# Moving the edge arrays' loads and packing ahead in the prologue of a four-layer graph network, and storing the packed edge table from the ScalarE queue

## The reference

```python
# layer 0: messages, mean over incoming edges, update
msgs = maximum(concat([h[src], h[dst], edge_attr]) @ mW1 + mb1, 0) @ mW2 + mb2
agg  = segment_sum(msgs, dst) / clip(count(dst), 1)
upd  = maximum(concat([h, agg]) @ uW1 + ub1, 0) @ uW2 + ub2 + h
x    = x + layernorm(upd) * gamma + beta
# layer 1: sum over neighbours;  layer 2: weighted GCN;  layer 3: APPNP step
x = x + h @ W1 + b1 + segment_sum(h[src], dst) @ W2 + b2
x = x + segment_sum(norm * (h @ W)[src], dst) + bias
x = x + h + relu(0.9 * segment_sum(norm1 * h[src], dst) + 0.1 * h)
```

## Time and profile before

| | |
|---|---|
| median of 3 runs | 1050.0 us (1049.88 to 1053.69) |
| the profiled execution | 1055.58 us, of which the span of the trace is 1053.7 us |
| PE busy | 877.1 us (83% of the span) |
| DVE busy | 645.6 us (61%) |
| ACT busy | 503.3 us (48%) |
| POOL busy | 495.6 us (47%) |
| DMA, mean over the span | 160 GB/s, 169.02 MB |

### The profile page before, as it was taken

One profiled execution on the slowest core, in us unless ns is written; L12 is line 12 of the kernel. 1 busy time (PEld: TensorE's weight loads), 2 busy tenths in 40 slices (PEclk: granted clock), 3 DMA queues, 4 the chain that ended last, 5 costly groups with the idle time before them and its releaser, 6 DMA issues.

```text
span 1053.7 us, 21016 instructions
## 1 busy us (share of the span) xinstructions
PE 877.1 (83%) x7797; PEld 792.2 (75%) x7797; DVE 645.6 (61%) x1759; ACT 503.3 (48%) x1012; POOL 495.6 (47%) x496
## 2 busy tenths in 40 slices
PE   4422887888778787888898888899899999999997
PEld 3422777777777776777887888788788988889786
DVE  5524676867776677667777777787775231213664
ACT  3211455655555555565666666676334300111874
POOL 6457665666666677566666666533411000003111
PEclk9566899999999999999999999999999999999999
DMA  5641355555655558555555555545623787786410
GB/s 145 193 135 45 96 147 147 151 151 149 202 160 147 147 139 138 160 152 157 153 152 148 155 159 153 143 144 169 187 62 141 283 306 285 292 304 206 136 54 23
DMA packets 118795, 169.02 MB, mean 160 GB/s; under 512 B 17248, under 2 KB 85382, under 8 KB 118691
## 3 DMA queue, kind: packets, MB, share of 16 engines
q1 hardware_dynamic: 104405, 138.82, 42.7%
q0 software_dynamic: 13648, 28.21, 10.9%
q10 hardware_dynamic: 638, 0.61, 0.3%
HBM read 109.15 MB, written 58.44 MB: 159 GB/s over the span
## 4 chain that ended last, share of the span: by engine, by line
PE 76%; issue 10%; DMA 4%; DVE 3%; another core or an unknown queue 2%; POOL 2%; ACT 2%; SPq 0%; ACTq 0%; DVEq 0%
PE ps L1883 13%; PE ps L1868 12%; PE ps L1740 12%; PE ps L1706 9%; PE ps L1720 9%; PE ps L1707 8%; PE ps L1738 4%; DMA edge_windows<-room 2%; PE ps L1693 2%; PE ps L1852 2%; POOL h L763 1%; PE ps L1755 1%; DMA x<-in_x 1%; DMA room<-dst_row 1%
## 5 line engine op out<-in xcount | busy, mean ns | idle before, releaser
L784 POOL DMA_INDIRECT room<-p_rows,idx x416 | 413.1, 993 | 235.2 <-issue 99.5
L1740 PE MATMUL ps<-room 128*128 128x100 bf16 x2400 | 193.8, 208 | 59.0 <-issue 57.5
L1740 PEld LDWEIGHTS ps<-room 128*128 128x128 bf16 x2400 | 152.0, 98 | 83.4 <-issue 79.2
L947 ACT ACTIVATE room<-ps 128x400 uint8<-128x400 f32 x200 | 101.1, 506 | 219.1 <-remote 209.6
L1706 PE MATMUL ps<-room,ident 128*128 128x128 f32 x832 | 172.0, 289 | 32.4 <-ACT g L922 15.4
L1738 PE MATMUL ps<-room 128*128 128x100 bf16 x800 | 155.6, 209 | 31.8 <-issue 29.2
L1707 PE MATMUL ps<-room 128*128 128x128 f32 x832 | 164.6, 280 | 0.4 <-issue 0.2
L1286 DVE TENSOR_TENSOR room<-room,Wp 128x800 bf16<-128x800 bf16 x300 | 156.4, 575 | 0.0
L1706 PEld LDWEIGHTS ps<-room,ident 128*128 128x128 f32 x832 | 129.8, 197 | 35.1 <-issue 31.3
L1279 DVE TENSOR_TENSOR room<-iota_k,Kt 128x800 bf16<-128x800 bf16 x100 | 57.4, 574 | 134.6 <-remote 134.4
L1883 PE MATMUL ps<-room,h 128*128 128x256 f32 (+1 forms) x650 | 136.2, 371 | 0.0
(11 more groups left out here) (195 smaller groups left out, 1096.9 us busy)
## 6 DMA issues: line engine op xcount, KB each, us to landing
weight_blocks<-room SPq DMA_DIRECT2D x100, 400.0 KB
room<-weight_blocks SPq DMA_DIRECT2D x12, 3200.0 KB
room<-dst_row SPq DMA_DIRECT2D x104, 128.0 KB
room<-count_blocks SPq DMA_DIRECT2D x8, 1600.0 KB
count_blocks<-room SPq DMA_DIRECT2D x100, 100.0 KB
room<-p_rows,idx POOLq DMA_INDIRECT x416
first_c<-count_blocks SPq DMA_DIRECT2D x4, 1600.0 KB
edge_windows<-room SPq DMA_DIRECT2D x1, 3328.0 KB
```

What stands on the lines that cost most here:

```text
L784: return pool.indirect_dma_start(to, None, table, bass.IndirectOffsetOnAxis(ap=at, axis=0))
L947: act.activation(cnt_out[:, u % OUTS, :, at16].rearrange("p h (b w) -> p b h w", w=4), of, ACT.Copy)\
L1740: weighed = pe.matmul(bank(6 + hh)[:, at], lo, movw[:, k, a, i, :, t], start=a == 0, stop=a == PARTS - 1)
```

## The change

The first instructions on four engines are put in another order.

- SP no longer loads `src`, `dst` and `w`. After `x` it loads `w_m1` and `prev_i`, then the attributes as before. The wait for `s_pad` 7 moves to the attributes' tail.
- ACT first computes the dummy square root that loads its table, then issues the loads of `src`, `dst` and `w`, each as 103 rows and one last row. After the roots of chunks 0 and 1 it waits for `s_pk` 2 and issues the store of the edge table; then it goes on with the chunks in a loop in which the root of chunk j + 2 stands behind `read_T0(j)`. It also makes `dst_b`, now a copy of `dst_r`.
- DVE memsets the paddings first, sets `sT` ahead of chunk 0, and casts and packs `src` and `dst` between the norm of chunk 0 and the statistics of chunk 1.
- POOL copies the weights behind the rows of chunk 0. The constants `zerob`, `iota_k`, `iota_l`, `npio` come after all the chunks' rows.
- SP's store of the edge table is gone, and with it the waits for `s_pk` and `s_pad`; the wait for the P rows stays.

```diff
 @block.sync
-            def tail(tile, array, arrived):
-                sp.dma_start(tile[QA:NQ - 1, 0:HALO], ...
-            def body(tile, array, arrived):
...
             sp.wait_ge(s_pad, 5)
             sp.dma_start(x[0:NR, NT - 1, :], x_in[128 * (NT - 1):N, :]).then_inc(x_of(NC - 1)[0], 16)
-            tail(src_l, src_in, s_src)
-            tail(dst_l, dst_in, s_dst)
-            body(w_l, ew_in, s_w)
-            tail(w_l, ew_in, s_w)
+            for k in range(2):
+                sp.dma_start(w_m1[:, k, :], mW1[k * D:k * D + D, :]).then_inc(s_wt, 16)
+            for q0, q1 in ((1, QA + 1), (QA + 1, NQ)):
+                sp.dma_start(prev_i[q0:q1, :], bass.AP(dst_in.tensor, q0 * QE - 2, [[QE, q1 - q0], [1, 2]]))\
+                    .then_inc(s_prev, 16)
...
-            sp.wait_ge(s_pad, 6)
+            sp.wait_ge(s_pad, 7)
...
             sp.wait_ge(s_eas, 16)
-            sp.wait_ge(s_pad, 7)
             for q in range(TS):
                 rows_of(q)
-            sp.wait_ge(s_pk, 2)
             sp.wait_ge(s_pt, 16 * NC)
-            sp.dma_start(win_tab.rearrange("(q j) c -> q j c", j=32), windows_of(pw_i)).then_inc(s_pst, 16)
 @block.gpsimd
             normed_rows(0)
-            pool.memset(zerob[:, :], 0.0).then_inc(s_con, 1)
-            normed_rows(1)
-            count_up(iota_k[:, :, :], ...); normed_rows(2); count_up(iota_l[:, :, :], ...)
-            count_up(npio[:, :], ...); normed_rows(3)
-            for j in range(4, NC):
-                normed_rows(j)
-            pool.wait_ge(s_w, 48)
+            pool.wait_ge(s_w, 32)
             pool.tensor_copy(pw[:, :, 1], w_l).then_inc(s_pk, 1)
+            for j in range(1, NC):
+                normed_rows(j)
+            count_up(npio[:, :], ...); count_up(iota_k[:, :, :], ...); count_up(iota_l[:, :, :], ...)
+            pool.memset(zerob[:, :], 0.0).then_inc(s_con, 1)
             pool.wait_ge(s_ea, 48)
 @block.scalar
-            for k in range(2):
-                act.dma_start(w_m1[:, k, :], mW1[k * D:k * D + D, :]).then_inc(s_wt, 16)
-            for tile, array, arrived in ((src_l, src_in, s_src), (dst_l, dst_in, s_dst)):
-                act.dma_start(tile[0:QA, 0:HALO], bass.AP(array.tensor, 0, [[QE, QA], [1, HALO]])).then_inc(arrived, 16)
-            act.wait_ge(s_pad, 1)
-            (the two loads of prev_i)
             act.wait_ge(s_con, 3)
             link(act.activation(sd[:, 0:1], eps[:, 0:1], ACT.Sqrt))
+            for n, (tile, array, arrived) in enumerate(((src_l, src_in, s_src), (dst_l, dst_in, s_dst), (w_l, ew_in, s_w))):
+                act.wait_ge(s_pad, n + 1)
+                act.dma_start(tile[0:NQ - 1, 0:HALO], bass.AP(array.tensor, 0, [[QE, NQ - 1], [1, HALO]]))\
+                    .then_inc(arrived, 16)
+                act.dma_start(tile[NQ - 1:NQ, 0:QR],
+                              array[(NQ - 1) * QE:E].rearrange("(a e) -> a e", a=1)).then_inc(arrived, 16)
...
-            pipeline((0, root(0, 0)), (2, read_T0(0)), (3, read_P))
+            root(0, 0)(0)
+            root(0, 0)(1)
+            act.wait_ge(s_pk, 2)
+            act.dma_start(win_tab.rearrange("(q j) c -> q j c", j=32), windows_of(pw_i)).then_inc(s_pst, 16)
+            for j in range(NC):
+                read_T0(0)(j)
+                if j + 2 < NC:
+                    root(0, 0)(j + 2)
+                if j:
+                    read_P(j - 1)
+                if j == NC - 2:
+                    act.wait_ge(s_dr, 1)
+                    act.activation(dst_b, dst_r, ACT.Copy).then_inc(s_dr, 1)
+            read_P(NC - 1)
 @block.vector
-            dve.memset(prev_i[0:1, :], -1).then_inc(s_pad, 1)
-            dve.memset(x[:, NT - 1, :], 0.0).then_inc(s_pad, 1)
             (memsets of src_l, dst_l, w_l)
-            dve.memset(ea_l[QA:NQ, :], 0.0).then_inc(s_pad, 1)
+            dve.memset(prev_i[0:1, :], -1).then_inc(s_pad, 1)
+            dve.memset(x[:, NT - 1, :], 0.0).then_inc(s_pad, 1)
+            dve.memset(sT[96:128, :, :], 1.0).then_inc(s_pad, 1)
+            dve.memset(ea_l[QA:NQ, :], 0.0).then_inc(s_pad, 1)
...
-            for j in range(NC):
+            dve.wait_ge(*x_of(0))
+            variance(0, 0, x)(0)
+            norm(0, 0)(0)
+            dve.wait_ge(s_src, 32)
+            dve.tensor_copy(src_f, src_l).then_inc(s_srcf, 1)
+            dve.wait_ge(s_dst, 32)
+            link(dve.tensor_copy(dst_f, dst_l))
+            dve.wait_ge(s_srcf, 1)
+            dve.scalar_tensor_tensor(pw_i.rearrange("p (e f) -> p e f", f=2)[:, :, 0], dst_f, 4096.0, src_f,
+                                     ALU.mult, ALU.add).then_inc(s_pk, 1)
+            for j in range(1, NC):
                 dve.wait_ge(*x_of(j))
                 variance(0, 0, x)(j)
-                if j:
+                if j > 1:
                     norm(0, 0)(j - 1)
             norm(0, 0)(NC - 1)
-            (the casts of src and dst)
             dve.tensor_scalar(dst_r, dst_f[:, 0:QE], sq[0:NQ, 0:1], None, ALU.subtract).then_inc(s_dr, 1)
-            dve.tensor_scalar(dst_b, dst_f[:, 0:QE], sq[0:NQ, 0:1], None, ALU.subtract).then_inc(s_dr, 1)
...
-            (the packing, and the memset of sT)
```

More of the change, by code:

```diff
@@ L517, in _ @@
         def _(sp):
-            def tail(tile, array, arrived):
[L519 to L522, removed]
-            def body(tile, array, arrived):
-                sp.dma_start(tile[0:QA, 0:HALO], bass.AP(array.tensor, 0, [[QE, QA], [1, HALO]])).then_inc(arrived, 16)
             for j in range(NC - 1):
@@ L767, in _ @@
             normed_rows(0)
-            pool.memset(zerob[:, :], 0.0).then_inc(s_con, 1)
-            normed_rows(1)
[L770 to L774, removed]
-            for j in range(4, NC):
-                normed_rows(j)
-            pool.wait_ge(s_w, 48)
-            pool.tensor_copy(pw[:, :, 1], w_l).then_inc(s_pk, 1)
+            pool.wait_ge(s_w, 32)
+            pool.tensor_copy(pw[:, :, 1], w_l).then_inc(s_pk, 1)
+            for j in range(1, NC):
+                normed_rows(j)
+            count_up(npio[:, :], [[0, 1]], step=-1).then_inc(s_con, 1)
+            count_up(iota_k[:, :, :], [[1, KCOLS], [0, 2]], base=KBASE).then_inc(s_con, 1)
+            count_up(iota_l[:, :, :], [[1, 128], [0, 2]]).then_inc(s_con, 1)
+            pool.memset(zerob[:, :], 0.0).then_inc(s_con, 1)
             pool.wait_ge(s_ea, 48)
@@ L867, in link @@
                 act.wait_ge(s_act, links[0])
-            for k in range(2):
-                act.dma_start(w_m1[:, k, :], mW1[k * D:k * D + D, :]).then_inc(s_wt, 16)
-            for tile, array, arrived in ((src_l, src_in, s_src), (dst_l, dst_in, s_dst)):
-                act.dma_start(tile[0:QA, 0:HALO], bass.AP(array.tensor, 0, [[QE, QA], [1, HALO]])).then_inc(arrived, 16)
-            act.wait_ge(s_pad, 1)
-            for q0, q1 in ((1, QA + 1), (QA + 1, NQ)):
-                act.dma_start(prev_i[q0:q1, :], bass.AP(dst_in.tensor, q0 * QE - 2, [[QE, q1 - q0], [1, 2]]))\
-                    .then_inc(s_prev, 16)
             act.wait_ge(s_con, 3)
             link(act.activation(sd[:, 0:1], eps[:, 0:1], ACT.Sqrt))
+            for n, (tile, array, arrived) in enumerate(((src_l, src_in, s_src), (dst_l, dst_in, s_dst), (w_l, ew_in, s_w))):
[4 more added lines that the diff above has]
+                              array[(NQ - 1) * QE:E].rearrange("(a e) -> a e", a=1)).then_inc(arrived, 16)
             def root(n, r, parts=TILES):
@@ L1209, in _ @@
                 .then_inc(s_of, 1)
[L1210 to L1213, removed]
             for n, (b, to) in enumerate(((2, idx), (1, dstT))):
```

## The result

The change made the kernel slower: 1094.5 us (median of 4 runs, 1091.62 to 1095.97) against 1049.94 us for the kernel before on the same chip. The ratio on record is 1.0398, 95% interval [1.0376, 1.0421]; the two medians alone would give 1.042. The text uses the ratios of the record throughout. The prediction was 1036.7 us, on the other side, and 1094.5 lies far outside its range (1021 to 1046).

A forecast was written before the change was run, and what follows sets the result against it. The prediction took the late edge-table store, and the slackless chain behind it to the keys, to bound the prologue. POOL's idle 12.31 us plus a 1.0 us earlier start gave 13.3: 1050.0 - 13.3 = 1036.7 us, range 1021 to 1046.

The forecast's parts named there:

- The store itself: Edge table's store on ACT: w lands at 11 to 12 us, issue at 12.3, data from 13.3, 24 us sooner.
- the store's issue holds ACT: Rival, chance 0.06: the table store's issue holds ACT up to 22 us, delaying the chunks; +9 us, 1059.
- POOL's start: POOL's first gathers: start at 33.0 instead of 34.00, a gain of 1.0 us; bounds 31.0 and 38.
- P rows or DVE late: Rival, chance 0.11: POOL's gathers start at 38, gain 8.3 us, 1041.7; with DVE late as well, 1046.
- When it has landed: Edge table's store lands between 36.7 and 45.5, before POOL needs it at about 48; POOL's idle 12.31 us go.
- DVE beside POOL: Casts and pack beside POOL's rows could slow by 2.0 us each, POOL's start by some 4; taken as nothing.
- The sum: Idle 12.31 plus start 1.0 is 13.3 us: first window gather from 61.22 to 47.9, forecast 1036.7; chance 0.64.
- all of that order moves alike: ACT's unexplained waits of 5.36 and 10.40 us behind the keys stay as they are, tied to the work's order.
- the late signals go or shrink: Rival, chance 0.12: new order breaks their cause, such as POOL's unbroken gathers; up to 15.8 us more, 1021.
- What bounds the kernel now: Prologue: table store's 23.40 us landing leaves POOL idle 12.31 us, then a chain without slack through the keys.
- a shift of the keys by X shifts the end by X: Sweep behind the keys: runs at PE's pace from about 106 us, so time gained at the keys reaches the end.

The follow-up runs named there:

- a_split: The changed kernel with src, dst and w each loaded as 96, 7 and 1 rows instead of 103 and 1; 1063.17 us, ratio 1.0091.
- d_split_latestore: a_split with the edge table's store put back in SP's list behind the P rows; 1055.49 us, ratio 1.0012.
- i_windows_first: a_split with window gathers issued ahead of all others, and unpacking, the split of the weights and keys moved ahead of quad 0; ratio 1.0003.
- b_rows103: The kernel before with src, dst and w loaded as 103 rows and the last, ACT's loads behind the paddings; 1069.5 us, ratio 1.0163.
- m: The kernel before with POOL held to four quads ahead of pre instead of six, nothing else; ratio 0.9887.
- f_break: a_split with one more wait: POOL waits for the third pre before the window gathers; ratio 1.0056.
- c_hold: The kernel before with POOL stopped before the gathers of quad 3 until the third keys are read; 1071.58 us, ratio 1.0164.
- o_quarter_rows: a_split with gathers of 128 B rows instead of 512 B, so its messages differ from the reference's; ratio 1.0111.

## Why the prediction was wrong, step by step

*The store itself* failed first. The step put w's landing at 11 to 12 us from a sum of bytes at 243 GB/s and took the issues as free. Of the loads' new shape, 103 rows instead of 96 and 7, it said nothing. On one engine they held ACT for 31 us, w landed at 43.2 and the store left at 44.03 instead of 12.3. That is 3.1 of the 4.0% lost; the early store is 0.8 (1.0091 - 1.0012) and all the rest 0.1, which is within the noise. The rival "the store's issue holds ACT" had the right engine and the right kind of event, but named the wrong DMA: the store's issue took 0.97 us, the loads' 31. With the loads split, w landed at 13.8 and the store left at 15.44, 3 us behind the forecast; `dst` had come at 12.87, and chunk 1's root, which the store stands behind, at 15.43.

*POOL's start* failed in size: in a_split 45.0 against 33.0, beyond its late bound of 38 (without the store beside it, in d_split_latestore, 33.80). The bound took the store's share of the engines, but the P stores' landing went from 2.3 to 10.6 us, and SP's issues, which the step did not count, were held 13.69 us for five (8.01 without the store). (The rule of the Trainium skill that the step weighed, "DMA: Bandwidth & Descriptors", section "Queues, rings and completion order", pointed the right way; the trace agrees with it in direction, with 10.6 us against 2.3.) The rival "P rows or DVE late" named this mechanism, at a third of its size (4 us against 11).

*When it has landed* held: in i_windows_first, which stores as a_split does, the store took 25.86 us and landed at 39.79, between 36.7 and 45.5, and in a_split no engine waits for it. *DVE beside POOL* was rightly taken as nothing: a_split's casts took 0.48 each and the pack 0.81. The 2.48 us of `dst_b` go with POOL's copies, not with its rows: in b_rows103 the same instruction ran at 38.80, beside the rows and ahead of the copies (41.68), in 0.48.

*The sum* failed in its last term, "all of that order moves alike". The late signals do not follow the order of the work. They follow POOL's unbroken runs of gathers (m, f_break), and the idle 12.31 us that the sum booked as a gain were what cut a run in two: without them a_split has one run of 39 gathers. The rival "the late signals go or shrink" looked at the right suspect, POOL's run, with the wrong sign: the change made the run longer. Experiment m shows what the suspect was worth: with a shorter run the kernel before gains 1.1%.

From *What bounds the kernel now*, "a shift of the keys by X shifts the end by X" is refuted by m: the keys came 0.5 us later than before and the kernel was 1.1% faster. c_hold shows it the other way (keys 0.2 us sooner, 1.6% slower), and in i keys 21 us sooner gained nothing. What the sweep waited for besides the keys were the counts of `pre`. What does move the end is the start of the steady sweep, relu(8).

## What to carry to other kernels

Look at the outermost dimension of every DMA that a change touches before counting its bytes: 103 rows cost an engine's queue 31 us where 96 + 7 + 1 took 3.5. An early store is not free because it is hidden itself; ask which small transfers it stands beside and who waits for them. And where a wait has no named releaser, treat it as open: test what its neighbours do before booking idle time as gain. Here a shorter lead of the gathers, which looks like a loss of freedom, was the largest gain of any single edit that was tried (1.1%).

## What the runs showed of the hardware

PE's semaphore counts reach ACT, DVE and POOL up to 36 us after PE's records (92.71 to 129.17 in the changed kernel) while POOL issues an indirect gather each 1.25 us. When it pauses, ACT waits some 0.5 us for them (c_hold). In six traces (before, after, a_split, c_hold, f_break, m) the last late counts of POOL's long run reach their waiters 1.9 to 6.3 us after its end (m: 91.97 and 93.88; the changed kernel: 122.87 and 129.17); a few come within the run (a_split's relu(1), 74.62). PE's own instructions were also spaced out in that state, with idle time between them that the same instructions don't show in the kernel before (90.55):

```profile
120.05 0.27 PE L1716 MATMUL ps<-g 128*128 128x128 f32 x1 [1.08 <-issue]
122.14 0.27 PE L1689 MATMUL ps<-w_m,hT 128*128 128x128 f32 x1 [1.83 <-issue]
124.94 0.37 PE L1689 MATMUL ps<-w_m,hT 128*128 128x128 f32 x1 [2.53 <-issue]
```

It does not depend on the bytes gathered (o_quarter_rows). What path PE's counts and POOL's gathers share stays open: no run here separates the number of gathers from their descriptors. Whether PE's records or its counts are the true time is open too.
